# A recommendation tower on one core: layers two and three and the MLP scheduled 31 steps behind the gathers, not 39

## The reference, cut to what matters

```python
e = jnp.stack([tbl_i[ids[:, i]] for i in range(16)], axis=1)   # 2048 x 16 x 256
x, xk, outs = e, e, []
for i in range(3):
    z = jnp.einsum('bfe,bge->bfge', x, xk).reshape(B, 256, E)
    z = relu(jnp.einsum('bce,oc->boe', z, Ws[i]) + bs[i][None, :, None])
    z = jnp.sum(z, axis=-1)                     # B x 16
    outs.append(z)
    xk = jnp.broadcast_to(z[:, :, None], (B, 16, E))
h = jnp.concatenate([*outs, dense_ctx], axis=1)  # 2048 x 64
h = jnp.maximum(h @ W_top1 + b_top1, 0.0)        # 512
h = jnp.maximum(h @ W_top2 + b_top2, 0.0)        # 256
y = h @ W_top3                                   # 1
```

## Time and profile before

| | us |
|---|---|
| three runs | 627.8, 629.25, 632.08 (median 629.25) |
| the profiled execution | 628.34, of it 626.6 span from the first to the last instruction |
| TensorE clock over the span | 0.992 of full speed |
| busy: PE, DVE, POOL, ACT | 575.6, 499.5, 463.7, 455.3 |

### The profile page before, as it was taken

One profiled execution on the slowest core, in us unless ns is written; L12 is line 12 of the kernel. 1 busy time (PEld: TensorE's weight loads), 2 busy tenths in 40 slices (PEclk: granted clock), 3 DMA queues, 4 the chain that ended last, 5 costly groups with the idle time before them and its releaser, 6 DMA issues.

```text
span 626.6 us, 19391 instructions
## 1 busy us (share of the span) xinstructions
PE 575.6 (92%) x7936; PEld 328.8 (52%) x7936; DVE 499.5 (80%) x220; ACT 455.3 (73%) x1298; POOL 463.7 (74%) x565
## 2 busy tenths in 40 slices
PE   2878798999999999999999999999999999997776
PEld 1444454555646555564656555565556555554354
DVE  5999999999898988889898988889888888941000
ACT  2666777787878787877887787777878788765542
POOL 6999999999988788888888888788878787621000
PEclk9999999999999999999999999999999999999988
DMA  3322222222222212222212122212212222100000
GB/s 97 112 73 73 69 70 68 70 70 65 69 64 61 61 58 63 61 61 62 65 56 65 57 61 60 69 55 68 60 55 67 61 61 57 47 3 1 1 1 2
DMA packets 14794, 35.97 MB, mean 57 GB/s; under 512 B 5922, under 2 KB 6306, under 8 KB 14690
## 3 DMA queue, kind: packets, MB, share of 16 engines
q0 software_dynamic: 12288, 33.57, 18.8%
q1 hardware_dynamic: 2418, 1.16, 0.7%
HBM read 34.70 MB, written 0.01 MB: 55 GB/s over the span
## 4 chain that ended last, share of the span: by engine, by line
PE 82%; POOL 8%; issue 4%; ACT 3%; DMA 1%; DVE 1%; SPq 0%; POOLq 0%
PE sum_ps L503 35%; PE turn_ps L483 10%; PE wide_ps L555 10%; PE outer_ps L535 8%; PE wide_ps L572 6%; PE wide_ps L546 4%; POOL emb L257 4%; PE outer_ps L531 4%; PE wide_ps L563 3%; POOL prods L267 2%; POOL prods L217 2%; ACT relu_k L426 1%; PE sum_ps L521 1%; PE sum_ps L517 1%; DVE prods L217 1%
## 5 line engine op out<-in xcount | busy, mean ns | idle before, releaser
L217 DVE TENSOR_TENSOR prods<-turn_ps,emb_t 128x3360 f32<-128x3360 f32 x128 | 466.1, 3655 | 55.1 <-ACT emb_t L399 52.2
L257 POOL DMA_INDIRECT emb<-tables,rows_sb x256 | 252.2, 985 | 45.4 <-issue 34.5
L503 PE MATMUL sum_ps<-prods,w_sb 128*32 128x272 f32 x4096 | 265.0, 397 | 18.6 <-POOL prods L217 11.1
L503 PEld LDWEIGHTS sum_ps<-prods,w_sb 128*32 128x32 f32 x4096 | 136.4, 110 | 103.6 <-issue 39.6
L426 ACT ACTIVATE relu_k<-outer_ps 128x1024 f32<-128x1024 f32 x128 | 132.4, 1035 | 11.2 <-PE outer_ps L535 11.1
L416 ACT ACTIVATE relu<-sum_ps,bias_sb 128x120 f32<-128x120 f32 x256 | 90.6, 361 | 58.4 <-PE sum_ps L503 57.2
L267 POOL TENSOR_TENSOR prods<-emb_t 128x256 f32<-128x256 f32 x128 | 95.3, 745 | 46.3 <-ACT emb_t L399 45.1
L398 ACT COPY emb_t<-turn_ps 128x512 f32<-128x512 f32 x128 | 75.3, 589 | 71.3 <-PE turn_ps L483 71.3
L483 PE MATMUL turn_ps<-ident_sb,emb 128*128 128x128 f32 x512 | 84.6, 289 | 12.7 <-DMA emb<-tables,rows_sb 10.0
L483 PEld LDWEIGHTS turn_ps<-ident_sb,emb 128*128 128x128 f32 x512 | 55.1, 142 | 60.5 <-issue 57.6
L406 ACT ACTIVATE prods<-emb_t 128x512 f32<-128x512 f32 x128 | 81.5, 637 | 3.3
(11 more groups left out here) (41 smaller groups left out, 284.3 us busy)
## 6 DMA issues: line engine op xcount, KB each, us to landing
emb<-tables,rows_sb POOLq DMA_INDIRECT x256
w_sb<-w_top SPq DMA_DIRECT2D x1, 512.0 KB, 4.3
ids_sb<-ids_t SPq DMA_DIRECT2D x1, 128.0 KB, 2.1
h<-dense_t SPq DMA_DIRECT2D x1, 128.0 KB, 2.9
w_sb<-w_top SPq DMA_DIRECT2D x1, 128.0 KB, 3.1
ident_sb<-ident SPq DMA_DIRECT2D x1, 64.0 KB, 2.1
w_sb<-w_cols SPq DMA_DIRECT2D x1, 64.0 KB, 1.9
wp_sb<-w_proj SPq DMA_DIRECT2D x1, 32.0 KB
```

The lines of the kernel that those rows point to most:

```text
L217: eng.tensor_tensor(out, every, shifted, ALU.mult).then_inc(done, 1)
L257: nc.gpsimd.indirect_dma_start(out=emb[:, k % EMB_RING, t * E:(t + 1) * E], out_offset=None, in_=tables, in_offset=bass.IndirectOffsetOnAx ...
L503: last = nc.tensor.matmul(sum_ps[s * 2 * F:(s + 1) * 2 * F, 0:SUM_COLS], w_sb[:, c, odd, :], x[:, c, 2 * s + odd, :, :], start=c == 0 and ...
```

## The change

The table of lags is written anew, and with it the order on every engine. A group's last stage comes 31 slots behind its first, so that there are 152 slots.

- The four rounds of a layer become two (`TURNS = 2`), in consecutive slots. Each fills all 512 columns of its four banks: four bias matmuls of 512 columns, then two times four float32 matmuls of 256 columns; ACT empties them with one ReLU of 128x2048.
- `hidden2` leaves `wide_ps` and becomes two side stages, `h2a` and `h2b`, of 8 passes each, right behind the transposes, in the side columns of `sum_ps`, each with its own ReLU in the same slot.
- Each slot has one of these after its sums: a round of double size (slots 0, 1, 4, 5 of 8, counted from a multiple of eight), `proj` (2), `fold` of layer 1 (3), `fold` of layer 0 (6), `hidden1` (7). Before, a single round stood in each slot and the wide stage behind it in five of them.
- `turn_proj` and both `reduce_fields` come one slot behind PE's stage, not two.
- On PE waits are moved ahead and spread, so that no instruction has more than one: the gather's wait stands within the sums of the step before, those on `sum_ps`'s readers within the transposes. One semaphore per buffer counts the three other makers of products.
- ACT makes the squares last in the slot, behind `relu_pairs` and the side copy.
- Gathers start `LEAD = 4` steps ahead, not 3, with eight buffers, not six.

```diff
-EMB_RING = 6
+EMB_RING = 8
-PT_RING = 3
-CAT_RING = 4
-LEAD = 3
+PT_RING = 2
+CAT_RING = 2
+LEAD = 4
+HALF_G = 2
+TURNS = G4 // HALF_G
-PROJ, Z0_FIN, TURN_P, Z0_DIAG, Z0_SUM = 8, 9, 10, 10, 11
-Z_BUILD = (13, 24)
-ROUNDS = (14, 26)
-FOLD = (18, 30)
-REDUCE = (20, 32)
-Z_T, HIDDEN1, HIDDEN2, OUTPUT = 33, 36, 37, 39
+PROJ, Z0_FIN, TURN_P, Z0_DIAG, Z0_SUM = 10, 9, 11, 9, 10
+Z_BUILD = (11, 15)
+ROUNDS = (12, 16)
+FOLD = (14, 19)
+REDUCE = (15, 20)
+Z_T, HIDDEN1, HIDDEN2, OUTPUT = 21, 23, (25, 28), 31
...
             for slot in range(LAST_SLOT + 1):
...
                 take_turned(slot + 2)
-                if slot - 1 in WIDE_AT:
-                    relu_hidden(*WIDE_AT[slot - 1])
-                squares(slot + 2)
+                if (g := group_at(slot - 1, HIDDEN1)) is not None:
+                    relu_hidden1(g)
                 relu_pairs(slot)
                 if slot in SIDE_AT:
                     take_side(*SIDE_AT[slot])
+                squares(slot + 2)
...
             def turn(k):
...
-                    pe.wait_ge(gathered[k % EMB_RING], PAIR * 16 * (k // EMB_RING + 1))
-                    at_least(pe, emb_t_ready, 2 * (k - 1))
+                    if k < 2:
+                        wait_gathered(k)
                     at_least(pe, prods_dve, k - 1)
                     for i in range(PAIR * EC):
+                        if i == 2 and k - 3 in SIDE_AT:
+                            wait_side(pe, k - 3)
+                        if i == 3:
+                            wait_sums_read(k - 2)
...
             def sum_pairs(k):
...
-                    pe.wait_ge(squares_ready, k + 1)
-                    pe.wait_ge(prods_dve, k + 1)
-                    pe.wait_ge(prods_pool, 2 * (k + 1))
-                    wait_sums_read(k)
-                    wait_side(pe, k - 1)
+                    pe.wait_ge(prods_other[k % PRODS_RING], N_OTHER * (k // PRODS_RING + 1))
...
+                elif what in ("h2a", "h2b"):
+                    i = 0 if what == "h2a" else 1
+                    pe.wait_ge(h1_ready, H1 * (g + 1))
+                    for a in range(H1):
+                        last = nc.tensor.matmul(h2_ps, w2_sb[:, a, i * P:(i + 1) * P], h1[:, a * P:(a + 1) * P],
+                                                start=a == 0, stop=a == H1 - 1)
+                    last.then_inc(h2_done, 1)
...
             def outer_round(k, g, q):
...
-                for j in range(J):
-                    last = nc.tensor.matmul(outer_ps[:, j, 0:F * F], z_wide[j * R:(j + 1) * R, k, q, :],
-                                            y[j * R:(j + 1) * R, k, :, :], start=False, stop=True)
+                for h in range(HALF_G):
+                    for j in range(J):
+                        last = nc.tensor.matmul(outer_ps[:, j, h * F * F:(h + 1) * F * F],
+                                                z_wide[j * R:(j + 1) * R, k, q * HALF_G + h, :],
+                                                y[j * R:(j + 1) * R, k, :, :], start=False, stop=h == HALF_G - 1)
...
                 sum_pairs(slot)
+                by_32 = slot in WIDE_AT and WIDE_AT[slot][0] in ("proj", "fold0", "fold1")
+                if by_32:
+                    wide(*WIDE_AT[slot])
                 if slot in ROUND_AT:
                     outer_round(*ROUND_AT[slot])
-                if slot in WIDE_AT:
+                if slot in WIDE_AT and not by_32:
                     wide(*WIDE_AT[slot])
```

116 lines of the change are left out of this document (63 added, 53 removed).

## The result

| | before | after | forecast |
|---|---|---|---|
| median of four runs, us | 629.91 (627.8 to 632.08) | 614.33 (613.35 to 615.57) | 610 (598 to 624) |
| ratio to before | 1 | 0.9753 [0.9715, 0.9792] | |
| profiled execution / its span | 628.34 / 626.6 | 614.28 / 612.5 | 610.4 / 608.7 |

What follows compares the result with a forecast made beforehand. PE was taken as the bound, with POOL leading in the head. Last sums at 560.5 + 6.5 - 5.2 - 1.2 = 560.6 plus a 48.1 tail gave 608.7 of span, 610.4 of execution; forecast 610 us, range 598 to 624.

Steps and rivals of the forecast that it cites:

- Changeovers and PE alone: Middle: seven fewer shape changeovers save 0.85 us, an ended wait 0.42; PE alone needs 34.25 us for eight steps.
- Stall (1): Middle, slot 7 of 8: layer 0's reduction and following products need 4.3 us against 4.02; PE stalls 0.3.
- Stall (2): Middle, slot 3 of 8: turn_proj and following products need 4.6 us against 4.29; PE stalls 0.3.
- Stall (3): Middle: layer 1's reduction meets a slot of 4.7 us, so the stall is 0.
- stall (4): Middle: layer 0's fold waits for ACT's last double ReLU, 0.2 us (0 to 0.5).
- The double ReLU: ACT: one ReLU of 2048 was taken to cost 1.9 us.
- The head: Up to step 32, POOL the bound: extra gathers, z_spread and earlier PE load make step 32's sums 6.5 us later.
- From step 32 on: Middle: eleven times 0.47 = 5.2 us won up to step 120, and 1.2 over the last seven steps.
- The tail: After the last sums start: 43.1 us at full clock plus 5 for the lower clock, 48 against 66.1.
- A: Middle: DVE's rows stay ahead, so PE is not held; eight steps 34.25, kernel 601 us; chance 15%.
- B: Middle: ACT's double ReLU delays copies and PE; eight steps 37.9, kernel 644 us; chance 12%.
- C: Tail at half clock costs some 14 us, not 5: 619, or 623 with a late high clock; chance 13%.

Runs made afterwards that it cites:

- e8_h2_in_slot7: Changed kernel with LEAD = 3, waits back in front of the sums, and h2a, h2b, y in slots 4, 7, 1 of 8: 606.67 us.
- e1_reduce_later: Changed kernel with layer 0's reduction one slot later on DVE: 611.42 us, ratio 0.9721.
- e10_turn_proj0_later: Changed kernel with only the first group's turn_proj one slot later on DVE: 609.79 us, ratio 0.9677.
- e8b_only_h2_slot7: Changed kernel with only h2a, h2b, y moved to slots 4, 7 and 1 of 8: 607.39 us, ratio 0.9675.
- e2_lead3: Changed kernel with gathers 3 steps ahead again, eight buffers kept: 608.47 us, ratio 0.9689.
- e6_before_lead4: Kernel before the change with gathers 4 steps ahead and eight buffers: 630.12 us, ratio 1.0018.
- e3_waits_at_sums: Changed kernel with the waits for readers of the sums' bank back in front of the sums and side stages: 611.30 us, ratio 0.9738.
- e11_relu_longer: Changed kernel with a superfluous 128x512 ReLU on ACT ahead of each double ReLU: 634.92 us, ratio 1.0083.
- e5_before_fold_first: Kernel before the change with proj and folds ahead of the round, right behind the sums: 630.29 us, ratio 1.0032.
- e7_lag39: Changed kernel with the MLP stages z_t, hidden1, h2a, h2b, y eight slots later each: 615.23 us, ratio 0.9770.
- e4: Changed kernel with ACT's squares back ahead of the ReLUs of the sums: 620.46 us, ratio 0.9880.
- e9: e8_h2_in_slot7 with twelve extra unread transposes behind each of the tail's six double rounds: 603.94 us, ratio 0.9592.

## Why the prediction was right, and where it was not

**Changeovers and PE alone: right.** 34.16 against 34.25. The price of a changeover, taken as 0.12 with ends 0.10 and 0.16, was measured alone as 0.14.

**Stalls of the middle: right in sum, 0.72 against 0.8, and not each for itself.** Stall (1) was 0.39, not 0.3. The extra 0.1 is DVE's: the reduction started 320.99 - 320.62 = 0.37 behind the fold, not 0.13 (a figure for which the prediction shows no row), while the terms behind it came 0.13 shorter than their sum. Stall (2) was 0.16, not 0.3. Stall (3) was nil as forecast, stall (4) nil and not 0.2, and the transposes ahead of the first `h2a` lose 0.17 that had not been forecast. e8_h2_in_slot7 and e1_reduce_later show the mechanism of (1): more PE work in the slot takes the stall away, a later reader does not.

```profile
320.99 0.43 DVE L375 TENSOR_REDUCE z_cat<-wide_ps 128x16 f32<-128x256 f32 x1 [1.87 <-PE wide_ps L585]
```

**The double ReLU: right in size.** 1.889 against 1.9. The prediction weighed it with 0.3 us and 0.83 ns per element from the Trainium skill ("ScalarE: Activation LUTs", Rules for kernel authors), which is that row's rule for an activation whose bias is read through a pointer. This one has none. The page "ScalarE: Activation LUTs" of the Trainium skill (What ACT_TABLE_LOAD costs) gives 186 ns and 0.833 ns per element for the form with an immediate bias, an estimate of 1.89; the trace agrees with it, and not with the 2.0.

**The head: the step that failed.** The prediction priced it as "2.5 + 1.05 + 3.0 = 6.5", with "POOL is the bound there, and nothing hides it" and, for PE, "the full load of PE begins at slot 24, not 32". It came to 12.2. How much later than in before the sums of a step start:

| us | after | e10_turn_proj0_later | e8b_only_h2_slot7 | forecast |
|---|---|---|---|---|
| sums 8 | 3.3 | 3.2 | 2.2 | 2.5 |
| sums 16 | 6.6 | 3.6 | 4.2 | |
| sums 24 | 9.3 | 5.9 | 7.0 | 3.5 |
| sums 32 | 12.2 | 8.7 | 9.2 | 6.5 |

The first term is right: POOL's first product starts at 15.50 and not 13.03, and e2_lead3 and e6_before_lead4 give back or add 2.5 and 2.4. The last is right too: from sums 24 to 32 it was 2.9, not 3.0. The term between them failed: for all that happens from step 8 to step 24 the prediction had 1.05, and it came to 6.0. These are the windows between the sums of 16 and 24, of before and then of after:

```profile
75.98:106.81 30.83, 27.22 (x387) 15.23 (x387) 29.96 (x13) 22.96 (x70) 28.01 (x35) 1.00 0.24 70
```

```profile
82.61:116.07 33.46, 32.39 (x461) 17.96 (x461) 30.56 (x14) 25.33 (x70) 28.87 (x36) 1.00 0.23 65
```

PE is busy 32.39 of 33.46 us, where before has 27.22 of 30.83, and POOL 28.87. So the bound here is PE, not POOL: with the new lags slots 16 to 23 hold four double rounds, `proj`, both folds and `hidden1`. The load of PE is nearly full from slot 16 on, not from 24. That is 2.6 of the 5.7 us that were missed, and e10_turn_proj0_later has 2.3 of it too.

From sums 8 to 16 it was 3.35 us, of which the prediction had 1.05. Here 1.7 is the half-clock spell, which is chance as far as can be seen: of ten profiles with the same wait ahead of that place four have it. The 0.6 that is left, by subtraction, goes to DVE's order: the rule of the middle, that a stage read one slot later holds the products behind it, applies from the first `proj` on. These are PE's waits from 18 to 151 us:

```profile
PE turn_ps L501 <- ACT own L424: 6.0, 7, 0.9
...
PE turn_ps L501 <- DVE prods L222: 4.9, 5, 1.8
```

Two of these five waits for DVE are 1.8 us long, at 64.11 and at 82.02. The second, in the timeline:

```profile
77.59 0.66 PE L501 MATMUL turn_ps<-ident_sb,emb 128*128 128x128 f32 x4
...
82.02 0.66 PE L501 MATMUL turn_ps<-ident_sb,emb 128*128 128x128 f32 x4 [1.80 <-DVE prods L222]
```

This slot, 15, lasts 82.02 - 77.59 = 4.43 us, and the one in the middle that answers to it (7 of 8) 325.04 - 320.62 = 4.42. The slot of the first wait, 11, lasts 64.11 - 59.66 = 4.45, its counterpart (3 of 8) 342.46 - 338.00 = 4.46. DVE's chain sets the same length in head and middle. In the first group nothing of an older group fills the slot (slot 11 has no fold, slot 15 no `hidden1`), so PE's wait is long. What a wait costs is less than its length, since PE without it would wait for POOL at 3.68 a step, or for ACT: e10_turn_proj0_later takes the first wait away and gains 1.1 at once, and keeps the second, 1.55 there, and still needs only 0.4 us more from sums 8 to 16 than before. The 6.0 us of waits for ACT were moved and not removed by e3_waits_at_sums, so their price is open.

The last 0.8 is there at sums 8 already. e8b_only_h2_slot7, the same program up to that step, is 1.05 earlier there, so this too differs from one profile to another. Together 2.6 + 1.7 + 0.6 + 0.8, less 0.1 behind step 24, are 5.6 of the 5.7. A count of PE's stages slot by slot from 8 on, as was made for the middle, would have found the 2.6.

**From step 32 on: better than forecast.** 6.9 won up to step 120, not 5.2; over the last seven steps 0.9, not 1.2. The late last sums, 564.9 and not 560.6, are the 5.7 of the head less 1.7 for the middle, plus 0.3 for the last seven steps.

**The tail: right.** 47.6 against 48.1. Walked at full clock it was to take 43.1. The stages at half clock took 1.5 + 0.5 + 0.4 + 1.5 = 3.9 more than at full clock (fold, `y`, `hidden1`, fold), where 5 had been allowed; the walk itself would be 43.7.

**The rivals.** A (PE is not held) fell with the first view: PE's waits are there in each period. But e8b_only_h2_slot7 is a kernel of this kind, 34.45 for eight steps. B (ACT's double ReLU sets the pace) did not happen, and e11_relu_longer shows how near it was: 0.5 us more ahead of the end of that ReLU is past the break-even. C (the tail at half clock) happened in part. The 5 us allowed for it came to 3.9 in the one profile. That it came so near is partly luck: e8_h2_in_slot7 and e8b_only_h2_slot7 have the same stages in their tails, and these differ by 2.6 us. The granted clock of after is 1.00, 0.93, 0.50, 0.84 and 0.97 in the windows of 565, 575, 585, 590 and 600 us. e5_before_fold_first is what C looks like: a gain of 5.5 us in the body, all of it lost again in the tail.

**What the gain is made of.** It is 15.6 us between the medians and 14.1 between the two profiled executions, and the parts below are those of the second. The prediction put all of it down to the tail, with head and middle cancelling. The sum is 18.4 + 6.9 + 0.9 - 12.2 = 14.0, so head and middle do not quite cancel. The experiments tell parts apart: the squares' place is worth 6 to 8 us; the lead costs 2.4 in the traces (by the times 1.3 in before, which is not clear of noise, and 4.0 in after); the first group's `turn_proj` costs 1.8, and 3.5 with the spell; the spread waits and the MLP's shorter lag net nothing that can be measured. Of the tail's 18.4 us, 9.5 come back with the MLP's old lag in e7_lag39. The double rounds were not undone by themselves, so their share of the tail, in which four cycles of 1.87 per layer became two of 3.27, stays a reckoning: 0.94 per layer.

## What to carry to other kernels

When a reader on an in-order engine moves close to its producer, write down the shortest slot that this sets (hand-over + read + the work queued behind it + hand-over back; here 4.3 us by the rows, 4.4 measured). Then fill that slot of the producer with work that it has to do anyway, as `h2b` did here for 0.8%, rather than move the reader. Walk the head slot by slot too: count in which slot each engine first has its full load, since that is where the bound passes from one engine to another (here at slot 16, not 24). Its first slots have no filling of an older group, and one instruction of the first group cost 1.8 us to the end of the run. And never count a gain in the body without the tail's clock: once as much was lost there as had been won.

## What the hardware showed that was not expected

- A wait of PE can cost twice, or not. In after 1.82 us of idle time at 64 us was followed by sums at half clock (1.2 GHz), another 1.7 us. Ten kernels of the study have this wait, 1.82 or 1.83; four profiles show the spell behind it (after, e1, e3, e7) and six do not (e2, e4, e8b, e8, e9, e11). The closest pair is e7_lag39 and e8b_only_h2_slot7: one program up to there, sums 12 at 64.22 in both, and 0.50 from 66 to 68 us in the first. This is the window of the second:

```profile
66.00:68.00 2.00, 2.00 (x36) 1.25 (x30) 2.00 (x2) 1.68 (x7) 1.82 (x3) 1.00 0.25 70
```

  So neither the wait nor the program decides. Each kernel has one profile, and what does decide was not settled.
- Superfluous work on an engine that waits kept its clock at 1.00 in the tail and made the kernel 2.7 us faster by the medians of four runs each, with intervals that overlap.
- The same reduction starts 0.37 us behind the same fold in one kernel and 0.14 in another with the same order on both engines (0.69 where ACT's squares stand earlier). The cause is open.
